# Second RMS norm of a fused scan, attention and mixture layer: one loop over four blocks instead of two

## The reference

```python
def _rmsnorm(x, gamma):
    return gamma * x * jax.lax.rsqrt(jnp.mean(x * x, axis=-1, keepdims=True) + EPS)
...
x = x + (out @ Wo + bo)
h2 = _rmsnorm(x, gamma2)
gate = jax.nn.softmax(h2 @ Wg + bg, axis=-1)
combined = jnp.einsum('btd,edf,bte->btf', h2, We, gate)
return x + combined
```

## Time and profile before

| | us |
|---|---|
| median of 2 runs | 3815.37 |
| range of the runs | 3815.02 to 3815.72 |
| profiled execution | 3798.63 |
| its slowest core's span (core 1) | 3796.7 |
| PE, DVE, ACT busy in that span | 2512.6, 1467.7, 874.2 |

### The profile page before, as it was taken

The page is one execution under the profiler, slowest core; times in us unless marked ns, Lnnn a source line. Parts: engine busy times, 40 slices in busy tenths (PEclk is TensorE's granted clock), DMA queues, the critical chain, the costliest instruction groups (busy, mean ns, idle before and its releaser), DMA issues.

```text
span 3796.7 us, 35219 instructions; the slowest of 8 cores (3771.4 to 3796.7 us)
## 1 busy us (share of the span) xinstructions
PE 2512.6 (66%) x12352; PEld 1184.3 (31%) x12352; DVE 1467.7 (39%) x1841; ACT 874.2 (23%) x1642; POOL 79.9 (2%) x143
## 2 busy tenths in 40 slices
PE   3545766557775587745975569664696647965478
PEld 1223332233332333323432234332343223432234
DVE  1344323443334433344324543245432363233532
ACT  2232003321123202332023320232203421024210
POOL 0000000000000000000000000000000000000000
PEclk9756888758887688866888669885698857987579
DMA  8641681202321022300222003220042201412013
GB/s 170 137 100 45 133 198 57 100 12 78 133 104 52 23 89 111 129 26 23 111 111 111 23 23 133 111 89 23 23 155 89 103 9 45 154 68 89 1 66 112
DMA packets 44455, 319.70 MB, mean 84 GB/s; under 512 B 5048, under 2 KB 5304, under 8 KB 28928
## 3 DMA queue, kind: packets, MB, share of 16 engines
q0 software_dynamic: 35040, 283.53, 23.8%
q1 hardware_dynamic: 9248, 33.91, 2.3%
HBM read 301.07 MB, written 48.23 MB: 92 GB/s over the span
## 4 chain that ended last, share of the span: by engine, by line
PE 53%; DVE 19%; DMA 10%; ACT 7%; issue 6%; DVEq 3%; ACTq 1%; POOL 0%; POOLq 0%; SPq 0%
PE bank L1434 22%; PE bank L617 3%; PE bank L1148 3%; PE bank L837 3%; DMA w<-wscr 3%; DMA w<-we 3%; PE bank L1374 3%; PE bank L443 3%; PE bank L489 3%; DVE vpu L931 3%; DVE kpot L931 2%; DVE sstat L1032 2%; PE bank L966 2%; PE bank L969 2%; DVE xph L1042 2%
## 5 line engine op out<-in xcount | busy, mean ns | idle before, releaser
L1434 PE MATMUL bank<-qpg,w 128*128 128x512 bf16 x4096 | 915.1, 387 | 74.0 <-DVE qpg L1407 46.8
L1434 PEld LDWEIGHTS bank<-qpg,w 128*128 128x128 bf16 x4096 | 406.6, 100 | 591.1 <-issue 127.8
L1407 DVE TENSOR_TENSOR qpg<-xph,ybuf 128x4096 bf16<-128x4096 bf16 x64 | 282.4, 4423 | 499.1 <-PE bank L1434 499.1
L1451 ACT ACTIVATE acomb<-bank 128x512 f32<-128x512 f32 x64 | 38.2, 597 | 1130.3 <-PE bank L1434 1126.5
L1018 ACT ACTIVATE hfm<-bank,sstat 128x128 bf16<-128x128 f32 x512 | 139.0, 381 | 529.6 <-DVE sstat L992 529.6
L1065 PE MATMUL bank<-cpb_s,xph 128*128 128x128 bf16 x512 | 64.8, 307 | 246.3 <-DVE xph L1042 246.3
L525 PE MATMUL bank<-xph,w 128*128 128x512 bf16 x512 | 134.3, 409 | 127.2 <-DMA w<-wscr 65.1
L617 PE MATMUL bank<-ln1g,w 128*128 128x512 bf16 x512 | 129.6, 421 | 96.2 <-DMA w<-wscr 73.6
L916 PE MATMUL bank<-zb,wupb 64*128 64x512 bf16 x128 | 73.2, 584 | 156.4 <-DVE vpu L931 112.1
L931 DVE TENSOR_SCALAR kpot<-bank,cph_s 64x512 bf16<-64x512 f32 x128 | 95.1, 743 | 198.4 <-PE bank L916 194.5
L992 DVE TENSOR_REDUCE sstat<-bank 128x4 f32<-128x512 f32 x128 | 82.5, 686 | 200.5 <-PE bank L969 197.6
(11 more groups left out here) (139 smaller groups left out, 2921.4 us busy)
## 6 DMA issues: line engine op xcount, KB each, us to landing
w<-wscr POOLq DMA_DIRECT2D x105, 2048.0 KB, 8.1
wscr<-w POOLq DMA_DIRECT2D x15, 2048.0 KB, 9.4
w<-we POOLq DMA_DIRECT2D x8, 2048.0 KB, 20.1
out<-ybuf SPq DMA_DIRECT2D x16, 1024.0 KB, 4.0
slotA<-x SPq DMA_DIRECT2D x4, 2048.0 KB
slotB<-x SPq DMA_DIRECT2D x4, 2048.0 KB, 11.8
w<-w_inT POOLq DMA_DIRECT2D x1, 2048.0 KB, 27.3
w<-w_aT POOLq DMA_DIRECT2D x1, 2048.0 KB, 23.6
```

The costliest lines, as they stand in the source:

```text
L1407: r = v.tensor_tensor(qpg[:, (e % 2) * 4096:(e % 2) * 4096 + 4096] .rearrange("p (c q) -> p c q", q=512), h2v[:, :, :], ybuf[:, e * 512:(e ...
L1434: last_pe = pe.matmul(bk[:, :], wslice(wbuf, kc, mc), qpg[:, (e % 2) * 4096 + kc * 512: (e % 2) * 4096 + (kc + 1) * 512], start=(e == 0 an ...
```

## The change

`f_us` keeps its four squares and its four Identity activations, but all of the work on a block now stands in one loop body: square, drain, Ln on one column, drain, Exp on one column, drain, the two waits on PE (for `tmstage` to be free), Identity, and an increment of `s_se` with a token `h2wb` for this block. The drain ahead of the increment is gone. No other code reads `h2wb`; `h2w` is again the end of the fourth Identity.

```diff
                                  accum_out=sstat[:, S_SU2 + b:S_SU2 + b + 1])
-                s.drain()
-                s.activation(out=sstat[:, S_R3:S_R3 + 4], in_=sstat[:, S_SU2:S_SU2 + 4],
-                             func=AF.Ln, bias=cpf2[:, C2_E2:C2_E2 + 1],
-                             scale=cpf2[:, C2_ID:C2_ID + 1])
-                s.drain()
-                s.activation(out=sstat[:, S_R3:S_R3 + 4], in_=sstat[:, S_R3:S_R3 + 4],
-                             func=AF.Exp, scale=cpf2[:, C2_NH:C2_NH + 1])
-                s.drain()
-                s.wait_ge(s_pe.h, tok[("hT", t, NCH - 1)])
-                s.wait_ge(s_pe.h, tok[("wo", t, NCH - 1)])
-                for b in range(NBLK):
+                    s.drain()
+                    s.activation(out=sstat[:, S_R3 + b:S_R3 + b + 1],
+                                 in_=sstat[:, S_SU2 + b:S_SU2 + b + 1],
+                                 func=AF.Ln, bias=cpf2[:, C2_E2:C2_E2 + 1],
+                                 scale=cpf2[:, C2_ID:C2_ID + 1])
+                    s.drain()
+                    s.activation(out=sstat[:, S_R3 + b:S_R3 + b + 1],
+                                 in_=sstat[:, S_R3 + b:S_R3 + b + 1],
+                                 func=AF.Exp, scale=cpf2[:, C2_NH:C2_NH + 1])
+                    s.drain()
+                    s.wait_ge(s_pe.h, tok[("hT", t, NCH - 1)])
+                    s.wait_ge(s_pe.h, tok[("wo", t, NCH - 1)])
                     last_s = s.activation(out=tmstage[:, b * 1024:(b + 1) * 1024],
                                  in_=uview[:, b * 1024:(b + 1) * 1024],
                                  func=AF.Identity,
                                  scale=sstat[:, S_R3 + b:S_R3 + b + 1])
-                s.drain(); s_se.inc(last_s)
+                    s_se.inc(last_s)
+                    tok[("h2wb", t, b)] = s_se.n
                 tok[("h2w", t)] = s_se.n
```

## The result

| | us |
|---|---|
| median of 32 runs of the changed kernel | 3829.64 |
| median of 31 runs of the kernel before, on the same chips | 3808.99 |
| ratio of times | 1.0062, 95% interval 1.0044 to 1.0081 |
| span of core 0, the slowest of the profiled execution | 3827.7 |
| median span of each die, before | 3781.8 and 3781.6 |

The change costs 0.62%. On the 3815.4 us from which the prediction started that is 23.7 us, with an interval of 16.8 to 30.9.

The account below looks back on a forecast made before the run. No engine full: an engine-to-engine chain bounds it. Direct cost 8 x 1.74 = 13.9 us; with clock steps 16.5 + 1.74 = 18.2, so 3815.4 + 18.2 = 3833.6 us, range 3818 to 3843.

Parts of the forecast that it names:

- The price of a block and the pace: ACT's new loop: 3.19 us a block against blocks coming every 1.57, so ACT paces; 12.86 us a tile, before 11.12.
- The 0.93: ACT, each added pair of Ln and Exp: 0.45 us from Ln to Exp, 0.48 from Exp to Identity.
- Who waits for the end: PE's first transpose needs all four blocks, nothing reads single tokens; all 1.74 us a tile goes onto PE's wait.
- Cover: Claim that nothing hides the delay, in the last tile or in tile 0: 8 tiles x 1.74 = 13.9 us.
- the sum of 13.9: Direct cost on PE's wait for the scaled blocks: 8 tiles x 1.74 us = 13.9 us.
- 18.2: Forecast slowdown: steps in about 5 of 7 tile periods, 16.5 us, and 1.74 us for the first tile.
- What the clock makes of it: PE's granted clock turns 1.74 us a tile into nothing or 3.3 us per period; a step in about 5 of 7.
- the second of the two forms: PE's clock in the expert matmuls: the rise to full clock comes later, and more is lost.
- its rival: PE's clock rises stay, periods stay at 460.7: 0 to 3 us slower, 3815 to 3818; chance 0.12.
- the clock takes it up: Rival: rises stay in nearly all tiles, so PE's shorter slow part gives back half; 0 to 3 us, chance 0.12.
- The gain by a cheap loop: Rival on ACT: cheap small work shrinks the tail without growing the head; 3790, or at most 18 us gain; chance 0.05.
- table loads: Rival on ACT: each function change brings a 1.283 us load, total 3860; chance 0.05, shared with other alternation costs.

Follow-up runs that it names:

- run with transposes by block: Changed kernel, with PE transposing each block on its own token into four PSUM banks and gate logits in bank 2; ratio to before 0.9966.
- the batched order: Kernel before's order on ACT, PE waiting for all four blocks, but transposes by block into four banks and gate in bank 2; ratio to before 0.9961.
- one pair more: Kernel before plus one more Ln and Exp pair with its two drains in the tail, order unchanged; ratio to before 0.9993.
- the pair for the last block only: Changed kernel without Ln, Exp and their drains for blocks 0 to 2, which are scaled by an old column; ratio to before 0.9977.
- the two groups: Kernel before, interleaved as two groups of two blocks, with one Ln and Exp pair per group; ratio to before 0.9991.
- the version that is split in two: Kernel before in two groups of two blocks, DVE scaling blocks 0, 1 and 3, ACT block 2, transposes by block; ratio to before 0.9885.
- that run: Kernel before, batched, with ACT scaling blocks 0 and 1 and DVE blocks 2 and 3 after the Exp; ratio to before 0.9997.

## Why the prediction was right

*The price of a block and the pace.* 3.19 us was the step from square to square, and 3.19 us was measured; the stretch was 12.86 in the sum, 12.85 in the row, and 12.90 as the mean of all tiles. Ln and Exp on one column took 386 and 295 ns, as taken from four columns. The 0.93 holds for Ln, Exp, drains and waits together; a pair with its drains alone is 0.83.

*Who waits for the end.* PE's wait grew to 9.3 us a tile, as forecast. The run with transposes by block shows the other side of this step: with a reader for each token the same 12.9 us on ACT go with a faster kernel, though the batched order gains almost as much from the four banks.

*Cover.* The prediction found none, and named no second effect on the path up to the experts. There was one: the gate matmuls, 2.8 us in all, 0.35 a tile, slower since the short piece at 2.4 GHz now comes behind them. It was missing from the sum of 13.9, in which it would have made 16.8 (8 x 2.10 to the gate). The steps by which the prediction went from 13.9 to 18.2 cover it in the number; that the number held although this term wasn't seen is luck in part.

*What the clock makes of it.* The prediction said 0 or 3.3 for each period, a step in about 5 of 7. From before to after, 8 of 48 periods fewer stand near 457.5 and 25 more near 464: 33 steps in 48, the same share. The mean period grew by 2.36 us. So the size of the steps and their share were right. The mechanism behind them was right too, in the second of the two forms that the prediction gave: the rise came later, and more was lost. In the mean the experts start 47.57 us after the first square where they started at 45.34, and run at 1.2 GHz for 5.31 us where it was 4.39. But the prediction let the rise move in some tiles and hold in others; it moved in 46 of 48. The periods hold only 33 further steps, so the rest was given back elsewhere in the tile; where, was not followed.

The table bears this out: with one pair more (+0.5 us to the gate) and with the pair for the last block only (-1.2) the rise stays in nearly all tiles and the period moves by +0.8 and -0.1; with +2.9 and -6.2 it moves by one step and by two in all of them, and the period by +3.3 and -6.15.

*The size.* 18.2 us were forecast and 23.7 measured, with 18.2 inside the interval. The mean span of the eight cores in the two profiled executions, 3782.3 and 3805.1, differs by 22.8 us: 1.3 up to the first transposes of tile 0, 6.3 in the first period (498.7 to 505.0), 14.2 in the other six, 1.1 behind the last. The prediction had 1.74 for the first tile and nothing for the first period beyond a step. This period has the conversion of the weights in it. Over the kernels of the table its mean lay between 494 and 514 us, and followed their direct change only loosely: 514 for the two groups, whose direct change is nothing. And the profiled execution of before was a short one: over the three sets of its executions that are on record with all cores the mean span is 3791.5 to 3798.6. So part of the 6.3 us is likely chance between executions; how much stays open.

The prediction's range isn't of one piece: it gives the chance of 0.78 to 8 to 28 us, but lets the range begin at 3 us, where its rival ends.

*The rivals.* That the clock takes it up happened to the one pair more, at half the direct cost, where the rise stayed in 22 of 24 tiles, and not to the change. The gain by a cheap loop fell with the pair for the last block only, in its own terms: with no small work in three blocks the stretch did fall under that of before, and the pairs' price is what lifts it over. There were 18 table loads, as before.

## What to carry to other kernels

Splitting a batched step into blocks can pay only where someone reads the blocks one by one; with PE as the one reader the split into four was about even here. Without a reader, count what the split multiplies (here a pair of small activations with its drains and waits, 0.93 us each) against the idle time that it fills (0.42 us a block): what is left goes straight onto the waiting engine, however low the busy share of the splitting engine is. With readers (DVE for the scaling, PE for the transposes) the version that is split in two, and so pays the small work twice, was the best; its gain isn't parted from that of the third block on DVE, and a split into four with both readers wasn't run. And where the clock's rises move in steps, a small change in time can vanish in the slowest core's time or come out larger: look at where the rise stands, and at all cores.

## What the runs showed of the hardware that was not expected

- A square with a row sum and an Identity behind it overlap unless a drain stands between them: the Identity starts 1.06 us after the square, with the read of the sum (0.19 us) beside it; with the drain, the next instruction starts after 1.22. The two waits for PE stand between this square and this Identity too, and don't show in the 1.06.
- DVE scales 1024 float32 columns to bf16 by a column in 0.75 us, two in 1.41, where the expectation of that run took 1.1 each from a product of two tensors; L1462 of before, a product of two float32 tensors, takes 4.42 us for 4096 columns, 1.1 for 1024. The Trainium skill ("VectorE: DVE Perf Modes", Mode 2×_2P) says that an operation with one tensor source in SBUF runs at twice the rate even in float32, and one with two doesn't; the trace agrees in the direction, with 0.66 us for the second block against 1.1.
- A shift in time alone changed the speed of matmuls, and not in one direction. The gate logits matmuls are the same in four kernels; from the start of the first to the end of the last they take 3.09 us before, 2.75 with one pair more (0.8 us later), 3.43 in the changed kernel (1.8 later) and 3.48 with the pair for the last block only (1.6 earlier). What counts is how much of them lies in the short piece at 2.4 GHz, and this piece stays in its place or moves by a whole step of 3.3 us.
